# Thirty-two matmuls of the shared experts' down projection, issued 24 expert steps earlier in the last loop

## The chip, the cores and the metric

The kernel runs on one core of one Trainium2 chip, in one launch. Its engines are PE (TensorE, matmuls), DVE (VectorE), ACT (ScalarE), POOL (GpSimd) and SP (SyncE, which here only issues DMAs). The metric is the device time of the launch in microseconds, taken over several runs.

## The reference, cut to what matters

Four residual blocks follow one another on an input of 4 x 512 tokens with 512 features: attention, a mixture of 8 experts, a linear recurrence with layer norm, and a second mixture. Only the last is touched. It routes each of 2048 tokens to 4 of 64 experts, each of which takes at most 128 tokens, and adds two shared experts that see every token:

```python
xb = zeros((E, CAP, D)).at[eid, pos].set(flat[tok], mode='drop')        # E=64, CAP=128, D=512
h = silu(einsum('ecd,edh->ech', xb, Wg)) * einsum('ecd,edh->ech', xb, Wu)   # H=128
yb = einsum('ech,ehd->ecd', h, Wd)
y = yb[eid, minimum(pos, CAP - 1)] * (w * valid)[:, None]
out = zeros((N, D)).at[tok].add(y)                                       # N=2048
hs = silu(einsum('nd,sdh->nsh', flat, Sg)) * einsum('nd,sdh->nsh', flat, Su)
out = out + einsum('nsh,shd->nd', hs, Sd)                                # S=2, shared hidden 512
x = x + tanh(g_ffn[1]) * out
```

The router gives the experts very unequal numbers of tokens, and the kernel treats all 64 as full tiles of 128 rows.

## The kernel before

Everything up to `experts` (L1895) runs first: the three earlier blocks, the router, a table `tab1` in HBM with each expert's 128 rows, and the shared experts for the first three groups of 512 tokens. Of the fourth group only the hidden values are made (`hidden`, 8 chunks of 128 features by 512 tokens); its down projection is left to the loop of `experts`. It consists of 4 tiles of 128 tokens times 8 chunks: 32 matmuls at L2007, each 128 x 128 times 128 x 512, and 4 evacuations by DVE at L2058 into `x_sb`.

`experts` is a loop over i from -1 to 64, written out by hand on five engines. In step i:

- PE turns the rows of expert i+1 (4 transposes, L1992), makes the gate and up product of expert i (8 matmuls, L2000), then, if `back_at(i)` says so, one of the 32 shared matmuls (L2007), then the down product of expert i-1 (L2015). The profile holds two records for each of the wide matmuls and for each of those at L2000.
- ACT copies the turned rows out of PSUM (L2025) and applies the gate (L2029); DVE multiplies gate and up (L2038), finds tokens and weights (L2040 to L2044), and writes the weighted result of expert i-1 into one of 8 buffers of `y` (L2051). It may write a buffer only when the scatter that read it eight experts earlier has landed (L2049).
- SP loads ahead (L1892 and L1881): the three weights of expert i+11, 768 KB, once the down product of expert i-1 is made, and the rows of expert i+7, 264 KB. There are 12 weight slots.
- POOL scatters each expert's result with an indirect DMA that adds in HBM (L1970). Even experts go to the table `sums1` and odd ones to `out`, and the scatter of expert e waits for the landing of that of e-2, so two are in flight at most.

After the loop SP loads the part of `sums1` that belongs to the last 512 tokens (L1961), DVE adds `x_sb` to it (L2061), and POOL adds `sums1` and that part to `out` with four DMAs (L1977, L1979). It begins these once all 64 scatters have landed.

Where the 32 matmuls stand is set by one number, `BACK` (L1933), the step of the first one. Before, it is E1 - 4 - 4 * 8 = 28: one matmul in each of the steps 28 to 59.

Of the kernel before, what the change touches and what calls it, by code (L numbers as in the profile page):

```python
# [17 lines left out]
TPB = SEQ // P  # L18
# [3 lines left out]
E1, H1, TOP1, CAP1 = 64, 128, 4, 128  # L22
# [52 lines left out]
def build(nc, A, out):  # L75
    ctx = ExitStack()
    with ctx:
# [66 lines left out]
        with later:  # L144
            with staged:
                T["stage_gate"] = sb("stage_gate", [P, NSH, DB * HSH], F32, staged)

                T["y0"] = sb("y0", [P, TPB, 2, D], F32, staged)
                T["hidden"] = T["stage_gate"][:].rearrange("p s (n t) -> p (s n) t", t=SEQ)
                T["s_w1"] = [staged.enter_context(nc.semaphore(f"m1_loaded_{n}")) for n in range(W_RING)]  # L150

                T["w_sd"] = sb("w_sd", [P, NSH, DB, HSH], F32, later, "right")
                T["flat_hi"], T["flat_lo"] = (sb(n, [P, DB, SEQ], F32R, later, "right") for n in ("flat_hi", "flat_lo"))
                splits = ExitStack()
                T["w_hi"], T["w_lo"] = (sb(n, [P, NSH, 2, DB * HSH], F32R, splits, "right") for n in ("w_hi", "w_lo"))

                def ring():

                    splits.close()
                    T["w1"] = sb("m1_w", [P, W_RING - 3, 3, D], F32, later, "right")  # L160

                T["ring"] = ring
                middle(nc, A, T)
                experts(nc, A, T)
# [1730 lines left out]
def experts(nc, A, T):  # L1895
# [4 lines left out]
    with c:  # L1900
# [29 lines left out]
        back_full, back_read = sem("shared_back_full"), sem("shared_back_read")  # L1930
        pX, pH, pY, pB = bank[0:2], bank[2:4], bank[4:6], bank[6:8]
        CHUNKS = SharedExperts.CHUNKS
        BACK = E1 - 4 - TPB * CHUNKS  # L1933
        PARTS = 4
        tables = T["sums1"], T["out_rows"]
        rest = T["summary"]
# [3 lines left out]
        def back_at(i):  # L1940

            return divmod(i - BACK, CHUNKS) if 0 <= i - BACK < TPB * CHUNKS else None

# [120 lines left out]
class SharedExperts:  # L2064
# [3 lines left out]
    CHUNKS = NSH * HSH // P  # L2068
# [91 lines left out]
```

## Time and profile before

| | us |
|---|---|
| median of 3 runs | 1152.73 (1150.12 to 1153.39) |
| the profiled execution | 1150.12 |
| its span | 1148.4 |
| PE busy | 1042.9 (91%) |
| POOL busy | 542.9 (47%) |
| DVE busy | 665.3 (58%) |
| first scatter of the loop | starts at 889.51 |
| last PE instruction of the loop | starts at 1107.70 |

Times in the trace are counted from the start of the span. A row of the waits names the instruction that waited, and behind the arrow what released it. In a timeline the brackets hold the idle time of the engine before the instruction and its releaser. A DMA's share of the engines is a mean over the core's 16 DMA engines; rounded spans can carry it a little above 1.

### The profile page before, as it was taken

Reading aid. Unit: us, or ns where it says so; the run is one execution under the profiler, and the core shown is the slowest. Engines: PE = TensorE matmul, PEld = TensorE weight load, DVE = VectorE, ACT = ScalarE, POOL = GpSimd, SP = SyncE. Lnnn points to the kernel's source line nnn. Section 1 sums busy time; section 2 is a strip of 40 time slices with the busy share of each in tenths; the row PEclk is TensorE's granted clock in tenths of the full one; section 3 lists DMA queues with packets and bytes.
Section 4 is the critical chain, followed back from the end, with each engine's and each line's share of the span. In section 5 each row is a group of like instructions: output and inputs, shape, how many; then the busy total and the mean of one; then the engine's idle time right before and its main releaser. Section 6 shows DMA issues by size and latency. Waiting matters only on the chain. (4 is left out here: it accounts for less than half of the span.)

```text
span 1148.4 us, 18313 instructions
## 1 busy us (share of the span) xinstructions
PE 1042.9 (91%) x5324; PEld 730.8 (64%) x5324; DVE 665.3 (58%) x1533; ACT 472.4 (41%) x823; POOL 542.9 (47%) x509
## 2 busy tenths in 40 slices
PE   3999999999869999999799999999998999999960
PEld 2555555555426777777279568577587888777740
DVE  4677777776547888888488437358131444333330
ACT  2465565555417888888342031221211222222210
POOL 4444645545334666666542546356141434343551
PEclk9999999999979999999899999999999999999985
DMA  9965556753543333332540231033047999999737
GB/s 278 340 223 170 155 174 221 240 192 113 176 170 131 128 101 110 110 101 91 181 156 1 104 110 54 25 130 113 0 139 258 371 343 368 348 307 308 180 71 146
DMA packets 128138, 199.19 MB, mean 173 GB/s; under 512 B 35991, under 2 KB 44183, under 8 KB 128074
## 3 DMA queue, kind: packets, MB, share of 16 engines
q1 hardware_dynamic: 106826, 161.18, 41.8%
q0 software_dynamic: 20960, 36.70, 12.3%
q8 instruction: 32, 0.52, 0.2%
q10 hardware_dynamic: 288, 0.52, 0.1%
q14 instruction: 32, 0.26, 0.1%
HBM read 133.36 MB, written 87.03 MB: 192 GB/s over the span
## 5 line engine op out<-in xcount | busy, mean ns | idle before, releaser
L914 POOL TENSOR_TENSOR m_down_lo<-wo,m_down_hi 128x512 fp32r<-128x512 f32 x80 | 132.8, 1679 | 76.8 <-ACT m_down_hi L1009 76.8
L517 PE MATMUL bank<-win,vT 128*128 128x512 f32 x256 | 124.1, 598 | 0.0
L607 ACT ACTIVATE win<-bank 128x512 f32<-128x512 f32 x128 | 69.6, 595 | 109.4 <-PE bank L509 109.2
L677 DVE TENSOR_REDUCE negmax<-bank 128x1 bf16<-128x512 f32 x128 | 87.1, 681 | 43.7 <-PE bank L524 43.3
L1023 DVE TENSOR_TENSOR m_up_lo<-w,m_up_hi 128x1024 fp32r<-128x1024 f32 x80 | 99.3, 1242 | 12.9 <-ACT m_up_hi L981 11.5
L1970 POOL DMA_INDIRECT sums<-m_y,m_token x32 | 49.6, 1551 | 108.1 <-DMA sums<-m_y,m_token 64.9
L524 PE MATMUL bank<-k_hi,q_parts 128*128 128x512 f32 x128 | 76.5, 598 | 18.4 <-DVE negmax L677 15.0
L1235 POOL DMA_INDIRECT tab<-stage_up,slot x64 | 64.5, 1008 | 56.3 <-DVE slot L1570 38.3
L2000 PE MATMUL bank<-y,m_w 128*128 128x128 f32 x736 | 89.7, 275 | 0.0
L2000 PEld LDWEIGHTS bank<-y,m_w 128*128 128x128 f32 x736 | 86.4, 193 | 0.5 <-issue 0.5
L2102 ACT ACTIVATE sh_gate_a<-bank 128x512 f32<-128x512 f32 (+1 forms) x40 | 20.5, 513 | 154.8 <-PE bank L2095 117.4
L2116 PE MATMUL bank<-w_sd,stage_gate 128*128 128x512 f32 x192 | 83.7, 592 | 0.0
L2095 PE MATMUL bank<-flat_hi,w_hi 128*128 128x512 f32 (+1 forms) x320 | 74.4, 355 | 5.5 <-DVE stage_gate L2106 2.8
L407 POOL DMA_INDIRECT tab<-xn,slot x32 | 32.8, 1024 | 95.8 <-DVE slot L711 91.0
L2025 ACT COPY y<-bank 128x512 f32<-128x512 f32 x64 | 37.4, 586 | 93.8 <-PE bank L1992 87.8
L2095 PE MATMUL bank<-flat_lo,w_hi 128*128 128x512 f32 (+1 forms) x320 | 72.9, 349 | 1.4 <-issue 1.3
L2051 DVE TENSOR_SCALAR m_y<-bank,m_weight 128x512 f32<-128x512 f32 x64 | 48.0, 751 | 44.0 <-DMA sums<-m_y,m_token 18.9
L2095 PE MATMUL bank<-flat_hi,w_lo 128*128 128x512 f32 (+1 forms) x320 | 72.3, 348 | 0.0
L935 PE MATMUL bank<-m_up_hi,m_xT_hi 128*128 128x512 f32 x160 | 69.5, 434 | 2.6 <-DVE m_up_lo L1023 2.2
L1970 POOL DMA_INDIRECT out<-m_y,m_token x32 | 49.7, 1552 | 43.4 <-DMA out<-m_y,m_token 35.2
L2038 DVE TENSOR_TENSOR m_gh<-m_gh,bank 128x128 f32<-128x128 f32 x64 | 18.4, 288 | 88.5 <-ACT m_gh L2029 79.4
L524 PEld LDWEIGHTS bank<-k_hi,q_parts 128*128 128x128 f32 x128 | 25.0, 195 | 61.9 <-DVE negmax L677 50.9
(282 smaller groups left out, 2408.6 us busy)
## 6 DMA issues: line engine op xcount, KB each, us to landing
tab<-zeros SPq DMA_DIRECT2D x16, 1056.0 KB
m_w<-in_L_ffn_Wg SPq DMA_DIRECT2D x46, 256.0 KB
m_w<-in_L_ffn_Wu SPq DMA_DIRECT2D x46, 256.0 KB
m_w<-in_L_ffn_Wd SPq DMA_DIRECT2D x46, 256.0 KB
m_x<-tab SPq DMA_DIRECT2D x40, 256.0 KB, 2.7
ytab<-m_y SPq DMA_DIRECT2D x40, 256.0 KB, 2.1
stage_up<-tab SPq DMA_DIRECT2D x32, 264.0 KB
m_x<-tab SPq DMA_DIRECT2D x32, 264.0 KB
```

The lines of the kernel that those rows point to most:

```text
L517: nc.tensor.matmul(pO[s * 2 + h][:], vT[:, s, sb_, h:h + 2, :].rearrange("p a c -> p (a c)"), probs[:, sb_ % 2, h, :], start=(sb_ == 0), s ...
L524: nc.tensor.matmul(pM[:], q_parts[:, s, h, t * P:t * P + P], k_hi[:, s, h, :], start=True, stop=True).then_inc(pm_full, 1)
L607: nc.scalar.activation(probs[:, b % 2, h, :], pS[h][:], ACT.Exp, scale=1.0 / HEAD).then_inc(p_ready, 1)
L677: nc.vector.tensor_reduce(negmax[:, s, m:m + 1], pM[:], AX.X, ALU.max, negate=True).then_inc(pm_read, 1)
L914: nc.gpsimd.tensor_tensor(dn_lo[:, m, :], row(wo0, e * MB + m), dn_hi[:, m, :], ALU.subtract).then_inc(dn_lo_ready, 1)
L935: last = nc.tensor.matmul(pH[s][:], x[:, s, d, :], w[:, d, :], start=(d == 0 and part == 0), stop=(d == DB - 1 and part == 2))
L1023: nc.vector.tensor_tensor(up_lo[:, at, :], blocks(w01, e * DB + half * HALF, HALF), up_hi[:, at, :], ALU.subtract).then_inc(up_lo_ready, 1)
L1235: nc.gpsimd.indirect_dma_start(T["tab1"], bass.IndirectOffsetOnAxis(slot1[:, j, k:k + 1], 0), flat[:, j, :], None, bounds_check=E1 * CAP1 ...
L1970: nc.gpsimd.indirect_dma_start(tables[e % SUMS], bass.IndirectOffsetOnAxis(token[:, e % META:e % META + 1], 0), y[:, e % RING, :], None, b ...
L2000: last = nc.tensor.matmul(pH[s][:, k * CAP1:(k + 1) * CAP1], w[:, b, :], xT[:, s, b, :], start=(b == 0), stop=(b == DB - 1))
L2095: last = nc.tensor.matmul(out, w[:, k, wc], x[:, d, cols], start=(d == 0 and part == 0), stop=(d == DB - 1 and part == 2))
L2116: last = nc.tensor.matmul(pY[j][:], self.h[:, n, j * P:j * P + P], sd[:, s, b, :], start=(n == 0), stop=(n == self.CHUNKS - 1))
```

## The change

The number is set to 4. The 32 matmuls then stand in the steps 4 to 35, one in each, and the four evacuations at L2058 in the steps 12, 20, 28 and 36 instead of 36, 44, 52 and 60.

```diff
@@ -1930,7 +1930,7 @@
         back_full, back_read = sem("shared_back_full"), sem("shared_back_read")
         pX, pH, pY, pB = bank[0:2], bank[2:4], bank[4:6], bank[6:8]
         CHUNKS = SharedExperts.CHUNKS
-        BACK = E1 - 4 - TPB * CHUNKS
+        BACK = 4
         PARTS = 4
         tables = T["sums1"], T["out_rows"]
         rest = T["summary"]
```

On PE, at the steps 4 and 5 near the loop's beginning, the order before and now differs by the rows with a plus. `bank` is PSUM, `m_w`, `y` and `stage_up` hold weights of experts, `w_sd` and `stage_gate` those and the hidden values of the shared experts; a name in brackets is a semaphore that the row waits for.

```order
 L2000 MATMUL bank<-y,m_w 128x128 [waits m1_h_ready,m1_xT_ready]
 L2000 MATMUL bank<-y,m_w 128x128 x7
+L2007 MATMUL bank<-w_sd,stage_gate 128x512
 L2015 MATMUL bank<-m_w,m_gh 128x512 [waits m1_y_ready,m1_h_ready]
 L1992 MATMUL bank<-ident,m_x 128x128 [waits m1_xT_ready,m1_loaded_6]
```

The first shared matmul now stands in step 4, before the down product of expert 3, and it waits for nothing of its own.

On PE, at the steps 58 and 59 near the loop's end:

```order
-L2007 MATMUL bank<-w_sd,stage_gate 128x512
-L2015 MATMUL bank<-m_w,m_gh 128x512 [waits m1_y_ready,m1_h_ready]
-L1992 MATMUL bank<-ident,m_x 128x128 [waits m1_xT_ready,m1_loaded_0]
-L1992 MATMUL bank<-ident,m_x 128x128 x3
-L2000 MATMUL bank<-y,m_w 128x128 [waits m1_h_ready,m1_xT_ready]
-L2000 MATMUL bank<-y,m_w 128x128 x7
-L2007 MATMUL bank<-w_sd,stage_gate 128x512
 L2015 MATMUL bank<-m_w,m_gh 128x512 [waits m1_y_ready,m1_h_ready]
 L1992 MATMUL bank<-ident,m_x 128x128 [waits m1_xT_ready,m1_loaded_1]
```

The last 28 steps hold transposes, gate and up products and down products alone, as the first 28 did before; the other rows of this piece stand as they were, a few places further back.

On DVE, in step 12 of the changed kernel, the first evacuation of a shared tile:

```order
L2044 TENSOR_REDUCE m_weight<-m_match 128x1
L2051 TENSOR_SCALAR m_y<-bank,m_weight 128x512 [waits m1_added_1,m1_y_full]
L2058 TENSOR_SCALAR x_sb<-bank,gates 128x512 [waits out_begun,shared_back_full]
L2038 TENSOR_TENSOR m_gh<-m_gh,bank 128x128 [waits m1_y_full,m1_g_ready]
L2040 SCALAR_TENSOR_TENSOR m_match<-m_x,iota_e 128x4
```

Its wait for `out_begun` (four plain stores of `x_sb` to `out`) moves with it, from step 36.

## Rows read from the trace of the kernel before

**Rows 1.** The page's forty slices of the span: PE, and the DMA engines' busy tenths.
```profile
PE   3999999999869999999799999999998999999960
...
DMA  9965556753543333332540231033047999999737
```

**Rows 2.** Chain of waits, 1095 to 1149 us: start us, us, what.
```profile
1103.44 3.28 DMA out<-m_y,m_token
...
1107.97 4.84 DMA out<-m_y,m_token
...
1113.58 6.80 DMA out<-m_y,m_token
...
1121.01 2.82 POOL out L1977 x3
```

**Rows 3.** Timeline of PE in the loop: start us, us, engine, line, op, out<-in, count.
```profile
887.92 1.95 PE L2000 MATMUL bank<-y,stage_up 128*128 128x128 f32 x16
...
891.04 1.95 PE L2000 MATMUL bank<-y,m_w 128*128 128x128 f32 x16
...
1088.22 1.95 PE L2000 MATMUL bank<-y,m_w 128*128 128x128 f32 x16
...
1092.20 1.95 PE L2000 MATMUL bank<-y,m_w 128*128 128x128 f32 x16
...
1107.70 1.12 PE L2015 MATMUL bank<-m_w,m_gh 128*128 128x512 f32 x2
```

**Rows 4.** Stretches of the loop: us; busy us (count) by engine; PEclk, DMA share, GB/s.
```profile
900.00:965.00 65.00, 65.00 (x463) 55.33 (x462) 28.83 (x103) 18.14 (x42) 23.58 (x16) 1.00 1.07 361
1000.00:1062.00 62.00, 62.00 (x381) 47.52 (x380) 22.98 (x78) 13.54 (x31) 24.88 (x17) 1.00 1.01 310
1076.00:1082.00 6.00, 6.00 (x44) 5.05 (x44) 2.15 (x6) 1.45 (x3) 4.30 (x3) 1.00 0.48 90
1082.00:1108.00 26.00, 26.00 (x163) 20.11 (x163) 10.91 (x39) 5.74 (x14) 15.91 (x12) 1.00 0.31 42
```

**Rows 5.** Timeline of POOL, scatters 0, 20, 44, 48, 61 and 63.
```profile
889.51 1.61 POOL L1970 DMA_INDIRECT sums<-m_y,m_token  x1 [25.22 <-DVE m_y L2051]
...
972.91 1.55 POOL L1970 DMA_INDIRECT sums<-m_y,m_token  x1 [4.85 <-DMA sums<-m_y,m_token]
...
1062.36 1.55 POOL L1970 DMA_INDIRECT sums<-m_y,m_token  x1 [2.65 <-DMA sums<-m_y,m_token]
...
1076.36 1.55 POOL L1970 DMA_INDIRECT sums<-m_y,m_token  x1 [2.99 <-DMA sums<-m_y,m_token]
...
1107.97 1.55 POOL L1970 DMA_INDIRECT out<-m_y,m_token  x1 [0.30 <-issue]
...
1113.58 1.55 POOL L1970 DMA_INDIRECT out<-m_y,m_token  x1 [1.64 <-DMA out<-m_y,m_token]
```

**Rows 6.** Who waited for whom, 870 to 1149 us: us in total, times, longest us.
```profile
POOL sums L1970 <- DMA sums<-m_y,m_token: 64.9, 22, 5.7
...
DVE m_y L2051 <- DMA sums<-m_y,m_token: 18.9, 10, 3.5
...
DVE m_y L2051 <- DMA out<-m_y,m_token: 9.2, 6, 2.5
```

**Rows 7.** Timeline of SP's DMA issues: Wu of expert 37, Wd of expert 63, the end.
```profile
969.04 2.23 SPq L1892 DMA_DIRECT2D y<-in_L_ffn_Wu  x1
...
1068.91 0.43 SPq L1892 DMA_DIRECT2D m_w<-in_L_ffn_Wd  x1
...
1113.11 0.38 SPq L1961 DMA_DIRECT2D summary<-sums  x1
```

**Rows 8.** Timeline of DVE, weighting of experts 0, 3 and 61.
```profile
887.89 0.75 DVE L2051 TENSOR_SCALAR m_y<-bank,m_weight 128x512 f32<-128x512 f32 x1
...
897.24 0.75 DVE L2051 TENSOR_SCALAR m_y<-bank,m_weight 128x512 f32<-128x512 f32 x1
...
1105.56 0.75 DVE L2051 TENSOR_SCALAR m_y<-bank,m_weight 128x512 f32<-128x512 f32 x1
```

## The prediction

> **What bounds the kernel now.** The page first. PE is busy in nine tenths or more of nearly every slice up to the last two, and the DMA engines are busy in nine tenths or more of six slices in a row near the end [rows 1]. These six lie in the loop over the 64 experts, the only place that the change touches. There two things are near their limit at once.
>
> The table of stretches shows PE busy for all of 65.00 us between 900 and 965, for all of 62.00 between 1000 and 1062, and for all of 26.00 between 1082 and 1108 [rows 4]. Its granted clock is 1.00 in all of them, the 2.4 GHz level. In PE's timeline one step takes 891.04 - 887.92 = 3.12 us where it holds no shared matmul, and 1092.20 - 1088.22 = 3.98 us where it holds one [rows 3]. A shared matmul is thus worth 0.86 us wherever it stands in the loop, as long as PE waits for nothing.
>
> The DMA share is 1.07 at 361 GB/s in the early stretch, while PE goes at 3.12 us a step; 1.01 at 310 GB/s later, at 3.98 us a step; and 0.31 at 42 GB/s after the last weights [rows 4]. The scatters on POOL ride on these same engines. From expert 0 to 20 they come every (972.91 - 889.51) / 20 = 4.17 us, from 20 to 44 every (1062.36 - 972.91) / 24 = 3.73 us, and from 48 to 61 every (1107.97 - 1076.36) / 13 = 2.43 us [rows 5]. I call these the crowded, the middle and the free rate. The waits confirm that it is the DMA's own return that holds POOL: 64.9 us of waits for the landing of the scatter before on the even table alone [rows 6].
>
> So in the first part POOL falls behind PE by 4.17 - 3.12 = 1.05 us an expert, until the 8 buffers are full and DVE waits for landings: 18.9 us for the one table and 9.2 for the other [rows 6]. PE hides those, since it is never idle. SP feels the crowd too: issuing one load took 2.23 us at 969.04, against 0.43 at 1068.91 [rows 7]. In the middle POOL gains only 0.25 us an expert, and it catches up after the last weights.
>
> The chain of waits shows how near that is to the end: scatters at 1103.44, 1107.97 and 1113.58, each released by the landing of one before, and after the last landing the final adds at 1121.01 [rows 2]. The one load that stands between, at 1113.11 [rows 7], waits for the last even scatter and moves with it. Expert 61 was weighted from 1105.56 to 1106.31 [rows 8] and scattered at 1107.97, so POOL ends with a lag of under 2 us. The end of the kernel is set by the scatters' landing; PE, whose last matmuls start at 1107.70 [rows 3], has just stopped being the later of the two.
>
> **The change, part by part.**
>
> *PE.* 32 matmuls at 0.86 us leave the steps 28 to 59 and enter the steps 4 to 35: 27.5 us taken out and 27.5 put in, net 0. The first reads hidden values and weights that the block before has finished, and the order shows no wait on it. What hides nothing gains nothing: PE has no idle time in either place to be filled. If DMA starvation appeared in the new last part it would show here; weights are issued 11 steps, 11 x 3.12 = 34 us, ahead, and over 65 us of the same pace near the beginning PE never waited [rows 4]. I take 0.
>
> *DVE.* Four evacuations move 24 steps ahead, past nothing that DVE does not also do there. The wait for the four stores is one that POOL has behind it before its first scatter at 889.51 [rows 5], and step 12 comes later. Behind it on DVE stand the product for the next expert, and PE behind that, but they wait for nothing new; cost 0. The two PSUM banks of the shared tiles are used every 8 steps as before. Cost 0.
>
> *The position of the slow steps against the loads.* This is the term that remains. Before, 28 crowded steps were followed by 32 slow ones, seven of them (53 to 59) behind the issue of the last weights; POOL worked off its lag there. Now the slow steps come first, where POOL has no lag to work off, and the lag is built up in the steps 36 on, with less time left. Step by step:
>
> Expert 3 is weighted at 897.24 [rows 8], as before. Experts 4 to 35 then follow at 3.98, to be exact at (1092.20 - 1088.22), so expert 35 is weighted at 897.24 + 32 x 3.98 = 1024.6. Its scatter follows 1.6 us later if there is no lag (889.51 - 887.89 [rows 5, 8]): 1026. If all of the first 35 went at the crowded rate it would be at 889.51 + 35 x 4.17 = 1035.5. In between: at first loads are still catching up and the rate is the crowded one, then the middle rate of 3.73 wins back 0.25 us an expert. I take 1028, near the lower end, since 23 experts at the middle rate win back 5.8 us and some 12 crowded ones lose 12 x 0.19 = 2.3.
>
> The last weights: SP issued them at 1068.91 [rows 7], released by a step behind which seven shared matmuls still stood. These seven now stand ahead of it, so it moves to 1068.91 + 6.0 = 1074.9. The free rate began with the scatter at 1076.36; it moves to 1082.4. To this comes a backlog. Loads of 1032 KB, 1.057 MB, every 3.12 us are 339 GB/s; in the middle stretch they were 1.057 / 3.98 = 266 of the 310 GB/s, which leaves 44 for scatters. 339 + 44 = 383 against 361 moved at most [rows 4] leaves 22 GB/s over 17 steps or 53 us: 1.2 MB, 3.2 us at 361. Bounds 0 and twice that. I take 1085.
>
> Between 1028 and 1085 the scatters go at the crowded or the middle rate. The early stretch, the nearest row, had the same loads at the same pace and 4.17; I take 4.1, since it had a deeper backlog. 57 / 4.1 = 13.9, so POOL has then started expert 35 + 13.9 = 48.9. Expert 61 comes 12.1 x 2.43 = 29.4 us after that, at 1114.4, against 1107.97: 6.4 us later. What follows (landing, expert 63, the final adds from 1121.01 on) hangs on it and moves as a whole. The final adds themselves are unchanged.
>
> At 1085 PE is near expert 55, so the lag is about 6 of 8 buffers, and DVE does not wait.
>
> The bounds of this term. From below: no lag at expert 35 (1026), middle rate, free from 1082.4: 56.4 / 3.73 = 15.1, expert 50.1; 10.9 x 2.43 = 26.5; 1108.9, or +0.9. It can't go under 1106.6, since expert 61 is ready only at 1106.31: -1.4. From above: 1035.5, 4.17 and 1085: 11.9, expert 46.9; 14.1 x 2.43 = 34.3; 1119.3, or +11.3.
>
> The Trainium skill, "DMA: Bandwidth & Descriptors", section "Queues, rings and completion order", says that a DMA engine takes turns between the queue rows that have work, packet by packet. By that rule a scatter on POOL's queue does not stand behind all that SP has queued, and the depth of SP's backlog would not matter. The trace speaks partly against it: 4.17 at 1.07 share and 3.73 at 1.01 [rows 4, 5]. With the rule's reading, 3.73 from 1028 to 1085 gives expert 50.3 and 1111.0, 3 us later than before.
>
> **The forecast.** Sum 0 + 0 + 6.4, taken as +6. The profiled execution took 1150.12, its span 1148.4, and the median of the runs is 1152.73; I put the term on the median: 1158.7.
>
> **The rivals.**
>
> *A. POOL has caught up before the end after all* (not slower). Place: the steps 36 to 53. If scatters return there at the middle rate and no backlog forms, expert 61 is scattered between 1106.6 and 1108.9, and the time stays at 1152, from 1151.3 to 1153.6. It decides at a crowded interval under about 3.8 us. For it: the lag before was twice as deep and was still gone by the end. Against it: the early stretch with the same pace shows 4.17, and before there were seven slow steps behind the last weights, which are gone. Between A and the forecast lies a zone up to +3.5, which I count as A's.
>
> *B. POOL never catches up in the slow steps.* If the crowded rate holds over all the first 35 experts, the sum of the upper bound applies, +11.3: 1164. For it: 4.17 is over 3.98, and the initial fill of the weight slots takes time to drain. Against it: the rate of 3.73 in the same kind of steps.
>
> *C. The full ring of `y` cost PE something in the runs that the profile does not show* (faster). The median lies 2.6 us over the profiled run. If that were PE waiting at the buffers' filling near step 26, where the slow steps now prevent it, and POOL also caught up, it would be 1152.7 - 2.6 - 1.4 = 1148.7. Nothing in the rows shows such a wait.
>
> *D. The weights come late at the end and PE waits*, at steps 45 to 55: a deficit of 1.2 MB is 3 us of a lead of 34. It would need ten times that. I leave it 2 in 100, with B's time.
>
> **How the numbers follow.** Forecast (over +3.5 and up to +9): 0.54. A with its zone: 0.25. B and D, over +9: 0.14. C: 0.07, of which 0.05 is below -0.3%. A measurement of this kernel can tell about 0.3%, 3.5 us, from no change. Slower: 0.54 + 0.14 = 0.68. Faster: 0.05. Same: the rest, 0.27. The range for 8 in 10 leaves out the top of B and the bottom of A and C: 1152 to 1164. The forecast's own range is 1156.3 to 1161.7.
>
> **What the profile after would show.** PE's steps at 3.98 us from step 4 to 35 and 3.12 from 36 on, with PE's last matmul still at 1107.7: then the PE term is right. POOL's scatter 35 at about 1028, an interval of about 4.1 us up to 1085, and scatter 61 at about 1114, waiting for landings at each step: then the lag is right. The last weights issued at about 1075. DVE's waits for landings, 28.1 us before, mostly gone from the steps 20 to 30. The prediction is wrong if scatter 61 starts under 1110, or if PE shows idle time in the loop.

## The result and the profile after

The changed kernel takes 1159.1 us (median of 20 runs, 1152.28 to 1164.01) against 1151.48 before (20 runs, 1149.08 to 1159.47). The ratio is 1.0054, 95% interval 1.0042 to 1.0066: slower by half a per cent, 6.2 us (the two medians themselves lie 7.6 us apart). The forecast was 1158.7.

The profiled execution of the changed kernel is an unusually short one, 1147.57 us with a span of 1145.9, under that of the kernel before. It must therefore be read from its own first scatter. Here is POOL's timeline, scatters 0, 20, 27, 36, 45, 50, 61 and 63 of the loop (start us, us, engine, line, operation; in brackets the idle time before and its releaser). Four of them, 0, 20, 61 and 63, answer to [rows 5]:

```profile
881.55 1.61 POOL L1970 DMA_INDIRECT sums<-m_y,m_token  x1 [22.43 <-DVE m_y L2051]
...
959.59 1.55 POOL L1970 DMA_INDIRECT sums<-m_y,m_token  x1 [2.96 <-DMA sums<-m_y,m_token]
...
986.89 1.55 POOL L1970 DMA_INDIRECT out<-m_y,m_token  x1 [2.42 <-DVE m_y L2051]
...
1021.25 1.55 POOL L1970 DMA_INDIRECT sums<-m_y,m_token  x1 [1.56 <-DVE m_y L2051]
...
1056.39 1.55 POOL L1970 DMA_INDIRECT out<-m_y,m_token  x1 [1.95 <-DMA out<-m_y,m_token]
...
1077.00 1.55 POOL L1970 DMA_INDIRECT sums<-m_y,m_token  x1 [2.77 <-DVE m_y L2051]
...
1105.52 1.55 POOL L1970 DMA_INDIRECT out<-m_y,m_token  x1 [0.30 <-issue]
...
1110.97 1.55 POOL L1970 DMA_INDIRECT out<-m_y,m_token  x1 [1.42 <-DMA out<-m_y,m_token]
```

The first scatter starts at 881.55, 8.0 us earlier than in [rows 5]. Nothing ahead of the loop was changed, and in the thirteen profiles of this study that moment lies anywhere between 881.5 and 891.2. What the change moved is seen from there on: first to last scatter 1110.97 - 881.55 = 229.4 us, against 1113.58 - 889.51 = 224.1 before: 5.3 us more. The releasers change over the loop: scatter 27 waited 2.42 us for DVE, that is for its own expert; scatter 45 for the landing of scatter 43; and when scatter 50 starts, expert 54 has already been weighted.

Three rows of PE, SP and DVE, to be held against [rows 3], [rows 7] and [rows 8]:

```profile
1099.73 1.12 PE L2015 MATMUL bank<-m_w,m_gh 128*128 128x512 f32 x2
```

```profile
1068.72 0.43 SPq L1892 DMA_DIRECT2D m_w<-in_L_ffn_Wd  x1
```

```profile
1097.60 0.75 DVE L2051 TENSOR_SCALAR m_y<-bank,m_weight 128x512 f32<-128x512 f32 x1
```

PE's last matmuls start 1099.73 - 881.55 = 218.2 us after the first scatter, and 1107.70 - 889.51 = 218.2 before. PE lost nothing. The last weights are issued 187.2 us after the first scatter, 179.4 before. Expert 61 is weighted 216.1 us after it, as before, but is scattered at 224.0, against 218.5. The lag, from the end of the weighting to the scatter, is 7.2 us where it had been 1.7.

The stretches of the loop (us; busy us and count of PE, PEld, DVE, ACT, POOL; granted clock, DMA share, GB/s):

```profile
900.00:965.00 65.00, 65.00 (x389) 49.08 (x388) 24.23 (x86) 14.10 (x33) 26.36 (x17) 1.00 1.00 309
970.00:1000.00 30.00, 30.00 (x185) 23.01 (x184) 10.77 (x39) 6.77 (x16) 12.04 (x8) 1.00 0.92 283
1050.00:1075.00 25.00, 25.00 (x178) 21.23 (x177) 11.24 (x41) 6.91 (x16) 9.76 (x7) 1.00 1.07 361
```

From 900 to 965 the share is now 1.00 at 309 GB/s where it had been 1.07 at 361 [rows 4], then 0.92 at 283, and from 1050 on 1.07 at 361. The crowd has moved from the beginning of the loop to its end. The waits (us in total, times, longest):

```profile
POOL sums L1970 <- DVE m_y L2051: 57.0, 14, 22.4
POOL sums L1970 <- DMA sums<-m_y,m_token: 37.7, 15, 4.9
...
POOL out L1970 <- DMA out<-m_y,m_token: 27.2, 13, 3.6
POOL out L1970 <- DVE m_y L2051: 23.1, 11, 2.8
DVE m_y L2051 <- PE bank L2015: 22.3, 32, 0.7
```

POOL's waits for the landing on the even table fell from 64.9 to 37.7 us, but those for DVE on it rose to 57.0, of which 22.4 lie ahead of the first scatter. Not all of the rest is DVE's: the profile puts the waits of scatters 46 and 50 down to it too, although experts 49 and 54 had been weighted when these two started. DVE's waits for landings [rows 6] are gone. The chain that ended last (start us, us, what) runs from landing to landing:

```profile
1057.19 1.80 PE bank L2000 x16
...
1060.97 7.21 DMA sums<-m_y,m_token
...
1068.95 7.28 DMA sums<-m_y,m_token
...
1077.00 6.04 DMA sums<-m_y,m_token
...
1105.52 4.68 DMA out<-m_y,m_token
...
1110.97 6.88 DMA out<-m_y,m_token
```

The profile lets it leave PE at scatter 46, 179.4 us after the first, and before at scatter 59, at 1103.44 [rows 2] or 213.9 us. Neither point can be taken as it stands. Both scatters are put down to DVE, but their own experts had been weighted 3 us or more before, so what held them was the landing of the scatter two before. The weightings on DVE are the better measure. In the kernel before, at least one more expert had been weighted at the start of every scatter from 4 to 59. In the changed kernel that is so at only two scatters up to 40 (14 and 16), and at every one from 41 to 61. The lag that reaches the end is thus built up anew from about scatter 38 on. Scatters 61 and 63 take 4.68 and 6.88 us to land, as before.

### The profile page after: what moved, and what is told of

It reads as the page before. It is cut to its first block and busy times, and to the rows that moved or that the text cites. A ratio compares the mean times of both kernels' runs of the same rounds, so it can differ in the third digit from the quotient of the medians.

```text
span 1145.9 us, 18313 instructions
## 1 busy us (share of the span) xinstructions
PE 1040.6 (91%) x5324; PEld 731.6 (64%) x5324; DVE 664.2 (58%) x1533; ACT 472.2 (41%) x823; POOL 544.5 (48%) x509
## 5 line engine op out<-in xcount | busy, mean ns | idle before, releaser
L407 POOL DMA_INDIRECT tab<-xn,slot x32 | 32.8, 1025 | 96.0 <-DVE slot L711 91.1
L517 PEld LDWEIGHTS bank<-win,vT 128*128 128x128 f32 x256 | 47.1, 190 | 26.0 <-issue 15.1
```

Of the source, the lines that this page charges most:

```text
L517: nc.tensor.matmul(pO[s * 2 + h][:], vT[:, s, sb_, h:h + 2, :].rearrange("p a c -> p (a c)"), probs[:, sb_ % 2, h, :], start=(sb_ == 0), s ...
```

## The experiments

All starts below are counted from the first scatter of the same profile. In the table, each column is the time between two scatters on POOL in us, worked out from the timeline as above. Each ratio is to the kernel before, run beside it in the same session (its median was 1145.7 to 1153.9 us from session to session). The last four rows are kernels that leave work out.

| shared matmuls in steps | 0 to 20 | 20 to 36 | 36 to 50 | 50 to 63 | first to last | ratio to before |
|---|---|---|---|---|---|---|
| 28 to 59 (before) | 83.4 | 59.1 | 48.8 | 32.8 | 224.1 | 1 |
| 4 to 35 (changed) | 78.0 | 61.7 | 55.8 | 34.0 | 229.4 | 1.0054 |
| the same, again | 77.5 | 62.2 | 57.2 | 35.2 | 232.1 | 1.0048 |
| 20 to 51 | 81.9 | 55.5 | 50.9 | 34.7 | 223.2 | 0.9990 |
| 4 to 27 and 53 to 60 | 77.5 | 58.8 | 56.5 | 33.9 | 226.7 | 1.0026 |
| 12 to 43 | 81.0 | 53.3 | 54.9 | 36.0 | 225.1 | 0.9998 |
| spread over 0 to 58 | 79.4 | 58.7 | 53.0 | 32.9 | 224.0 | 1.0008 |
| 32 to 63 | 83.2 | 59.4 | 49.8 | 32.8 | 225.1 | 1.0007 |
| 20 to 51, last load behind the last scatter | 81.6 | 55.7 | 51.9 | 35.0 | 224.3 | 0.9977 |
| 4 to 35, lighter loads late | 78.1 | 61.6 | 51.2 | 33.6 | 224.5 | 1.0019 |
| 4 to 35, scatters 36 to 49 empty | 78.5 | 61.2 | 44.0 | 39.5 | 223.2 | 1.0004 |
| 4 to 35, four in flight | 77.5 | 62.2 | 43.7 | 40.3 | 223.6 | 0.9949 |
| 28 to 59, four in flight | 63.6 | 60.9 | 55.7 | 46.3 | 226.4 | 1.0005 |

The two stretches of the kernel before that no row above gives begin and end here (POOL's timeline, scatters 36 and 50 of the kernel before):

```profile
1032.00 1.55 POOL L1970 DMA_INDIRECT sums<-m_y,m_token  x1 [1.50 <-DMA sums<-m_y,m_token]
...
1080.80 1.55 POOL L1970 DMA_INDIRECT sums<-m_y,m_token  x1 [0.95 <-DVE m_y L2051]
```

**The changed kernel again, `BACK = 4`.**

> The changed kernel once more, beside the kernel before. Theory: the whole difference lies between the first and the last scatter of the loop, 229.4 us in the changed kernel's profile (881.55 to 1110.97) against 224.1 before (889.51 to 1113.58), and comes from the scatters' lag at the end; here 229 to 230 again, wherever the loop begins, and a ratio near 1.005. Rival: the first scatter of the changed kernel's profile came 8 us earlier than before's, so if the change also moves what stands ahead of the loop, it begins near 881.5 here too.

Ratio 1.0048 (1.0030 to 1.0066). POOL's timeline, scatters 0, 50 and 63:

```profile
888.59 1.61 POOL L1970 DMA_INDIRECT sums<-m_y,m_token  x1 [25.19 <-DVE m_y L2051]
...
1085.54 1.55 POOL L1970 DMA_INDIRECT sums<-m_y,m_token  x1 [0.30 <-issue]
...
1120.69 1.55 POOL L1970 DMA_INDIRECT out<-m_y,m_token  x1 [1.84 <-DMA out<-m_y,m_token]
```

The loop begins at 888.6, so its early beginning in the other profile was chance and the rival is out. First to last scatter is 232.1 us, a little over what was expected: 8.0 more than before. The two profiles, 5.3 and 8.0 us, bracket the 5.5 and 6.2 us that the two ratios give.

**All shared matmuls ahead of the last weights, but late.**

```diff
-        BACK = 4
+        BACK = 20
```

> The shared matmuls in the steps 20 to 51, all of them ahead of the issue of the last weights, as in the changed kernel, but late. Theory A: what costs is that no slow step is left behind the last weights (seven before), so that the last weights are issued 6 us later; first to last scatter 228 to 230 us, ratio 1.004 to 1.006, as with the first at step 4. Rival B: what costs is the length of the fast stretch in which the lag is built up at the end, 12 steps here against 28; then first to last scatter 225 to 227 us, ratio 1.001 to 1.002.

Ratio 0.9990 (0.9968 to 1.0011). POOL's timeline, scatters 0, 36, 50 and 63:

```profile
886.08 1.61 POOL L1970 DMA_INDIRECT sums<-m_y,m_token  x1 [25.14 <-DVE m_y L2051]
...
1023.56 1.55 POOL L1970 DMA_INDIRECT sums<-m_y,m_token  x1 [2.36 <-DMA sums<-m_y,m_token]
...
1074.50 1.55 POOL L1970 DMA_INDIRECT sums<-m_y,m_token  x1 [1.13 <-DMA sums<-m_y,m_token]
...
1109.24 1.55 POOL L1970 DMA_INDIRECT out<-m_y,m_token  x1 [0.98 <-DMA out<-m_y,m_token]
```

223.2 us from first to last, less than either theory gave, and 0.9 less than before. Theory A is false: no slow step stands behind the last weights here, and nothing is lost. B's direction is right. Scatter 36 comes 137.5 us after the first, 2.2 sooner than in the changed kernel (139.7), and from 36 to 50, where the steps are slow ones, the scatters take 50.9 us instead of 55.8.

**Twenty-four early, eight at the end.**

```diff
-            return divmod(i - BACK, CHUNKS) if 0 <= i - BACK < TPB * CHUNKS else None
+            return divmod(AT.index(i), CHUNKS) if i in AT else None
-        BACK = 4
+        AT = list(range(4, 28)) + list(range(53, 61))
```

> 24 of the shared matmuls in the steps 4 to 27 and the last 8 in the steps 53 to 60, so that eight slow steps stand behind the issue of the last weights (seven before), and 25 fast steps stand ahead of it. Theory A (slow steps behind the last weights decide): first to last scatter 223 to 225 us, ratio 0.999 to 1.001. Rival B (the lag built in the long fast stretch decides): 228 to 230 us, ratio 1.004 to 1.006.

Ratio 1.0026 (1.0005 to 1.0047), 226.7 us, between the two. POOL's timeline, scatters 36, 50 and 63; the first is at 888.44:

```profile
1024.74 1.55 POOL L1970 DMA_INDIRECT sums<-m_y,m_token  x1 [0.94 <-DMA sums<-m_y,m_token]
...
1081.19 1.55 POOL L1970 DMA_INDIRECT sums<-m_y,m_token  x1 [0.30 <-issue]
...
1115.12 1.55 POOL L1970 DMA_INDIRECT out<-m_y,m_token  x1 [1.98 <-DMA out<-m_y,m_token]
```

Scatter 50 is 192.8 us after the first, 1.5 later than before and 2.7 earlier than in the changed kernel. The eight slow steps at the end change nothing after scatter 50: 33.9 us, as in the changed kernel. What they may have given lies ahead of it, since the last weights are through sooner; the run does not separate that from the slow steps' own effect.

**Four scatters in flight, first shared matmul at step 4 and at step 28.**

```diff
-SUMS = 2
+SUMS = 4
-        tables = T["sums1"], T["out_rows"]
+        tables = T["sums1"], T["out_rows"], T["tab0"], T["ytab0"]
```

> The changed kernel with four tables for the scatters in place of two, so that four are in flight and each waits for the one four experts earlier. The results of the experts with e mod 4 of 2 or 3 go to two dead tables and are left out of the output; the final adds are unchanged in size. Theory: the pace of the scatters is set by the return of each under load, so with four in flight the lag is gone: scatter 61 starts within 1 us of its expert's weighting, first to last scatter about 221 to 223 us, ratio 0.995 to 0.999 to the kernel before. Rival (the DMA engines' bandwidth or PE sets the end): 228 us or more, as in the changed kernel.

> The kernel before (first shared matmul at step 28) with four tables, four scatters in flight, and the same results left out as in the run with four tables and the first at step 4. Theory: without the lag the place of the shared matmuls is worth nothing: first to last scatter within 1 us of the other's 223.6, ratio to the kernel before 0.994 to 0.997 as there. Rival: the early place costs something besides the lag, and this one is 3 us or more below the other.

Early: ratio 0.9949 (0.9934 to 0.9965), 223.6 us. From the first steps on, scatters wait for DVE and no longer for landings: with four in flight the lag is gone, and so is what the early place costs. Late: ratio 1.0005 (0.9983 to 1.0027), 226.4 us, against what was expected. The wait rows of PE's weight loads say why, first of the early, then of the late kernel:

```profile
PEld bank L1992 <- DMA stage_up<-tab: 2.8, 3, 1.1
```

```profile
PEld bank L1992 <- DMA m_x<-tab: 4.5, 4, 2.0
...
PEld bank L1992 <- DMA stage_up<-tab: 2.1, 2, 1.1
```

PE now waits for rows of experts (`tab` is their table): 2.8 us and 6.6 us. The waits lie in the fast steps of each, from 1084 to 1092 us in the early kernel and from 938 to 970 in the late one. PE's last matmuls come 219.3 and 222.1 us after the first scatter, not 218.2. With two in flight no such wait shows in either kernel. I take it that scatters which are not held back take their part of the DMA engines, and that loads are then late where steps are fast. That is a miss of the theory, which had PE safe in both. The ratios of the two differ by 6.4 us, the spans after the first scatter by only 3.2 (256.8 and 260.0); the rest stays unexplained.

**Lighter loads at the end, `BACK = 4`.**

```diff
-        sp.dma_start(slot[:, k, :], w).then_inc(T["s_w1"][n], 16)
+        if k == 2 and e >= 44:
+            sp.dma_start(slot[:, k, 0:16], w[:, 0:16]).then_inc(T["s_w1"][n], 16)
+        else:
+            sp.dma_start(slot[:, k, :], w).then_inc(T["s_w1"][n], 16)
```

> The changed kernel, with the down-projection weights of the experts 44 to 63 loaded in part only: 16 of 512 columns, so 520 KB in place of 768 KB for each of these; the products with the rest use what the slot held before, and the output of these experts is not the reference's. Theory (the scatters' return is slow in the fast stretch because the loads fill the DMA engines): the interval from scatter 38 to 50 falls from 4.13 us to PE's 3.12, POOL has no lag, and first to last scatter is 221 to 224 us; ratio to the kernel before 0.997 to 1.000. Rival (the scatters of this stretch are slow of themselves, since the experts 36 to 42 have full tiles): the interval stays over 3.8 us and first to last scatter over 227.

Ratio 1.0019 (1.0002 to 1.0036), 224.5 us. The last scatter comes 4.9 us earlier than in the changed kernel, a little less than the theory gave; but the interval from scatter 36 to 44 is still 31.1 / 8 = 3.9 us, and only from 44 to 50 does it fall, to 3.3. Both theories have a part: the engines moved 300 GB/s in the first of these stretches, against 332 in the changed kernel, and the scatters came hardly sooner.

**Empty scatters in the same stretch, full loads.**

```diff
+                rows = nobody[:, 0:1] if 36 <= e < 50 else token[:, e % META:e % META + 1]
-                    tables[e % SUMS], bass.IndirectOffsetOnAxis(token[:, e % META:e % META + 1], 0), y[:, e % RING, :], None,
+                    tables[e % SUMS], bass.IndirectOffsetOnAxis(rows, 0), y[:, e % RING, :], None,
```

`nobody` is a column of row numbers out of range.

> The changed kernel, whose scatters of the experts 36 to 49 are still issued and waited for, but with every row number out of range, so that they add nothing (the results of these experts are left out of the output). Loads and PE are as in the changed kernel. Theory (the loads alone make each scatter's return slow): from scatter 38 to 48, 3.7 to 4.1 us each, and scatter 50 comes at 193 us or later after the first. Rival (full tiles, 128 rows for most of the experts 37 to 42, fill the DMA engines): from scatter 38 to 48, 3.12 us each, PE's pace, and first to last scatter 221 to 224 us.

Ratio 1.0004 (0.9978 to 1.0029), 223.2 us. POOL's timeline, scatters 39, 40, 50 and 63, and below it the stretch from 1050 to 1075:

```profile
1040.29 1.55 POOL L1974 DMA_INDIRECT out<-m_y,m_nobody  x1 [1.56 <-DVE m_y L2055]
1043.40 1.55 POOL L1974 DMA_INDIRECT sums<-m_y,m_nobody  x1 [1.56 <-DVE m_y L2055]
...
1074.94 1.55 POOL L1974 DMA_INDIRECT sums<-m_y,m_token  x1 [1.35 <-DMA sums<-m_y,m_nobody]
...
1114.47 1.55 POOL L1974 DMA_INDIRECT out<-m_y,m_token  x1 [1.05 <-DMA out<-m_y,m_token]
```

```profile
1050.00:1075.00 25.00, 25.00 (x177) 21.17 (x176) 11.15 (x40) 6.98 (x17) 12.10 (x9) 1.00 1.01 339
```

Scatter 40 follows 39 after 3.11 us and waits for its expert. From 38 to 48 the interval is 3.14 us, as the rival had it. The loads are all there, 339 GB/s and a share of 1.01, and yet scatter 50 comes 183.7 us after the first, at PE's heels. My theory is false in this part: loads alone leave room for empty scatters at PE's fast pace. In the changed kernel the written rows come on top, and the engines are at 361 GB/s and 1.07 in this stretch. Counted from the reference's own inputs, the experts 37 to 42 all have 113 to 128 rows, and of the experts 15 to 34 only four have more than 87. As an estimate, a full tile is 128 rows of 2 KB or 0.262 MB, at one in 3.12 us 84 GB/s, and 339 + 84 is well over the 361 of the fullest stretch shown. The stretch shown is that of the experts 44 to 49, with 46 rows on the mean; that it is still full I put down to what the full tiles before it left over, which no run shows by itself.

A scatter's own rows are the lesser part of its time. By the same count expert 16 has 2 rows, and in the kernel before its scatter went out at 956.46 in the crowded stretch:

```profile
956.46 1.55 POOL L1970 DMA_INDIRECT sums<-m_y,m_token  x1 [5.06 <-DMA out<-m_y,m_token]
...
964.66 1.55 POOL L1970 DMA_INDIRECT sums<-m_y,m_token  x1 [4.79 <-DMA sums<-m_y,m_token]
```

Scatter 18 had to wait for its landing and came 8.20 us after it; behind the full tile of expert 14 it was 8.63. Of that kernel's scatters 4 to 25 that were waited for, the five with under 20 rows took 7.5 us on the mean, the eight full ones 8.6. Among the empty ones of this run, those that were waited for took 6.05 to 6.82 us in the same measure. So a nearly empty tile returns late too where the engines are overfull; whether bytes or the number of written rows fill them, no run separates.

**The steps 12 to 43, an even spread, and the last 32 steps.** Edits: `BACK = 12`; `AT = [n * 58 // 31 for n in range(TPB * CHUNKS)]` with `back_at` as in the split; `BACK = 32` with a `dve.drain()` ahead of L2060.

> The shared matmuls in the steps 12 to 43. Theory C: scatters take about 4.13 us where steps are fast and loads run, 3.55 where steps are slow, as long as POOL has a lag to work off; slow steps in which it has none are lost, as in the steps 21 to 35 of the changed kernel, where each scatter waited for its expert. Here the lag of 12 fast steps lasts through most of the slow ones, so fewer are lost: scatter 50 comes 190 to 194 us after the first (188.4 with the first matmul at 20, 195.5 and 197.0 at 4), first to last 225 to 228 us, ratio 1.001 to 1.003. Theory A (slow steps behind the last weights): as with 4, 229 or more.

> The 32 shared matmuls spread evenly over the steps 0 to 58, in a bit more than every second one, so that a step takes 3.58 us on average from the first to the last. Theory C: loads ask for 295 GB/s all the time and never fill the DMA engines, the scatters return in under 3.75 us an expert with a small lag throughout, and POOL is at PE's heels when the last weights are in: scatter 50 before 186 us after the first, first to last 221 to 223 us, the floor that PE sets; ratio 0.997 to 1.000. Rival: PE's end is the floor before already, and nothing can be seen: 223 to 225.

> The shared matmuls in the last 32 steps, 32 to 63 (with one drain on DVE before its last addition). The fast stretch of 32 steps fills the 8 buffers near step 26; theory: DVE then waits for landings at 4.17 us a step while steps ask for 3.12, so PE waits 1.05 us in some five of the steps 27 to 31, first to last scatter 226 to 230 us, ratio 1.002 to 1.005. Rival A (slow steps behind the last weights are what helps; eleven here): at or under 224, ratio at or below 1.000.

Ratios 0.9998 (0.9984 to 1.0013), 1.0008 (0.9993 to 1.0023) and 1.0007 (0.9989 to 1.0025): none can be told from the kernel before. With 12, scatter 50 comes at 189.2 and the last at 225.1, the one a little sooner than theory C had it, the other at its lower bound. The spread gives 224.0, inside its rival's range, and scatter 50 came at 191.1 and not before 186. But the rival's reason, that PE's end was the floor already, isn't shown. Two of the spread's shared matmuls stand in the steps 0 and 1, ahead of the first scatter, so PE's last matmuls start 216.7 us after it and not 218.2, and the last scatter follows 7.3 us behind them, against 5.9 before and 5.0 with the steps 20 to 51. A lag of up to three experts stayed up to scatter 53. With 32, DVE waits for landings more than twice as long as before [rows 6]:

```profile
DVE m_y L2051 <- DMA out<-m_y,m_token: 35.4, 14, 3.6
...
DVE m_y L2051 <- DMA sums<-m_y,m_token: 27.5, 14, 3.8
```

That is 62.9 us, and still PE's last matmuls start 218.4 us after the first scatter. The expected stall of PE did not come; a step of slack between DVE and PE takes waits of up to 3.8 us.

**A candidate: step 20, and the load behind the last scatter.**

```diff
-            sp.wait_ge(added[0], 16 * E1 // SUMS)
+            for s in range(SUMS):
+                sp.wait_ge(added[s], 16 * E1 // SUMS)
```

> The first shared matmul at step 20, and SP's load of the last part of sums1 waits for the last scatter of both tables instead of the even one alone. In all runs the last scatter takes 6.8 us to land while this load of 1 MB runs beside it, and about 4.8 where none does. Theory: it lands 2 us sooner, and the four final adds, which together take 27 us of DMA time, begin 2 us sooner; the load and DVE's addition (8.2 us) still end before the fourth add's turn, so the kernel is 2 us faster than with step 20 alone: ratio 0.996 to 0.999. Rival: the load only moves behind and competes with the adds, and nothing is gained.

Ratio 0.9977 (0.9954 to 1.0001). The chain of waits at its end:

```profile
1115.05 4.95 DMA out<-m_y,m_token
...
1120.07 5.43 DMA summary<-sums
...
1125.53 2.30 DVE summary L2062
...
1128.12 1.33 POOL out L1980
```

The last scatter now lands in 4.95 us, as expected, against 7.37 with step 20 alone, but the load, DVE's addition and the fourth add follow one another and carry the chain. From the last scatter to the end of the span it takes 34.8 us, 35.5 with step 20 alone: of the 2.4 us, 0.7 are left. From the first scatter to the end of the span it takes 259.0 us, 258.6 with step 20 alone and 258.9 before. The ratio lies in the range expected, but its interval overlaps that of step 20 alone, so the runs can't tell the two apart. No version that does all the work beats the kernel before beyond its interval.

## Why the prediction was right, point by point

*PE: net 0.* Right, to 0.1 us: 218.2 from the first scatter to PE's last matmuls in both.

*DVE and the moved wait: 0.* Right; no wait for the stores shows, and DVE's waits for landings vanished.

*The scatters' lag moves to the end: +6.4.* Right in kind and size. The prediction named as its own sign of being wrong a scatter 61 that starts under 1110. Read literally the profile shows that, 1105.52, but only because its loop began 8.0 us early; from the first scatter it is 224.0 us, which on the clock of the profile before is 1113.5, and in the second profile of the changed kernel it started at 1115.1. Counted from the first scatter, the terms were:

| term | predicted | measured |
|---|---|---|
| scatter 35 | 138.5 | 136.6 (1018.14 - 881.55) |
| last weights issued | 185.4 | 187.2 |
| interval in the crowded stretch | 4.1 | 3.92 (35 to 50); 4.13 from 38 on |
| scatter reached at 195.5 | 48.9 | 50 |
| interval after it | 2.43 | 2.59 (50 to 61) |
| scatter 61 | 224.9 | 224.0 |

POOL had no lag left from scatter 22 on, the lower bound of that term; the last two misses (one expert further, each interval 0.16 longer) cancel in part. The 6.4 became 5.5 on scatter 61, and 8.0 in the second profile. That the forecast of 1158.7 lies within 0.4 us of the median is luck in part: it was put on a median of three runs, 1152.73, and that of twenty is 1151.48.

*The cause inside that term was only half right.* I named two: seven slow steps lost behind the last weights, and a lag rebuilt in fast steps. The first is refuted as a cause of its own. With none behind them (20 to 51) nothing is lost, with eleven (32 to 63) nothing is won, and with eight (split) half of the loss remains. The table shows where it lies: from scatter 36 to 50, +7.0 us. The steps 20 to 36 cost +2.6, since POOL, without a lag, goes at PE's slow pace there; 0 to 20 give 5.4 back, and 50 to 63 cost +1.2. That the lag is the whole of it, two runs show: with four in flight, or with empty scatters from 36 to 49, it is gone, and so is the loss (223.6 and 223.2 us, against 224.1 before). The table bears out that slow steps shorten the time only where POOL has work waiting; no run tests that by itself.

*The crowded rate comes from the loads.* Incomplete. The early stretch of 4.17 held full tiles too; with empty scatters the same loads allow PE's pace, 3.14. The backlog sum (339 + 44 against 361) had the right form, but its 44 GB/s for scatters is an average that hides full and empty tiles.

*What I drew from the Trainium skill's rule on taking turns between queue rows* ("DMA: Bandwidth & Descriptors", section "Queues, rings and completion order"), a pace of 3.73 and +3, was not borne out: the interval was 3.92 from scatter 35 to 50 and 4.13 from 38 on. The rule itself is not refuted by that; no run here tests it.

*The rivals.* A (caught up) is what the other places show, not this one. B did not come: only the first 16 scatters came near the crowded rate, at 4.05 us each. C has nothing for it. D did not come with two in flight; it did, in a small way, with four.

## What to carry to other kernels

Where long steps can be placed freely on one engine, they are best placed where the DMA demand of the loop peaks and where a queue has work waiting; long steps over a queue that waits for its input are lost. Here a bad place cost half a per cent, and no place beat the one before. Then find the floor: with the first step at 12, 20, 28 or 32 the last scatter comes 5.0 to 6.9 us behind PE's last matmuls, against 11.2 and 13.9 in the two profiles with 4, so there is little left above PE's own end. Compare stretches from a mark inside the profile, not from the launch.

## What was not expected of the hardware

With the same instructions ahead of it, the loop began between 881.5 and 891.2 us in thirteen profiles, taken on more than one chip, a spread of 9.7 us that hides a 5 us effect in a single one. An indirect DMA whose rows are all out of range still took its 1.55 us on POOL. Fourteen of them in a row, two in flight, kept PE's pace beside loads of 339 GB/s, though each that was waited for took 6.05 to 6.82 us until the next on its table started, where those in the first profile of the changed kernel took 7.5 to 8.7 from scatter 38 to 50. And with four scatters in flight in place of two, PE waited 2.8 and 6.6 us in all for rows, and with two never.
